# Row sums of a masked attention moved from POOL additions to a ScalarE exponential, and the next input loaded into dead buffers

## The reference, cut to what matters

```
f0: norm_adj @ (x @ W) + bias                          # norm_adj = d^-1/2 adj d^-1/2
f1: 8 heads of 32; softmax over q.k/sqrt(32) where adj != 0, else -inf;
    @ v @ w_proj + b; plus a scaled layernorm of that result
f2: 3 steps of a gated unit: a = adj @ h; z, r = sigmoid(..); h = (1-z) h + z tanh(..)
f3: 8 heads of 32; softmax over q.k/sqrt(32) - 1e9 (1 - adj); @ v @ Wo + b
```

## Time and profile before

| what | value |
|---|---|
| median of 3 runs | 2841.97 us |
| lowest and highest | 2840.41, 3499.7 us |
| profiled execution | 2836.56 us |
| its span, first to last instruction | 2834.8 us |
| mean granted TensorE clock | 0.967 |

### The profile page before, as it was taken

The page is one execution under the profiler, slowest core; times in us unless marked ns, Lnnn a source line. Parts: engine busy times, 40 slices in busy tenths (PEclk is TensorE's granted clock), DMA queues, the critical chain, the costliest instruction groups (busy, mean ns, idle before and its releaser), DMA issues.

```text
span 2834.8 us, 50080 instructions
## 1 busy us (share of the span) xinstructions
PE 2594.9 (92%) x16825; PEld 2007.0 (71%) x16825; DVE 2463.6 (87%) x5962; ACT 1686.0 (59%) x3559; POOL 1474.8 (52%) x1787
## 2 busy tenths in 40 slices
PE   7878989999999998989989899998989989898997
PEld 6556767777776776767777677777767777676775
DVE  7978889899898988989899898998988889889676
ACT  4434755748466574755747467474665746545677
POOL 2756456445745546565455654446555464657312
PEclk8889999999999999999999999999999999999999
DMA  5211202212031121202212031121301222021022
GB/s 142 45 26 23 59 18 61 50 38 59 20 77 31 38 59 47 65 18 50 59 40 59 18 68 42 39 59 34 69 26 37 59 53 59 18 48 36 12 46 68
DMA packets 93231, 132.80 MB, mean 47 GB/s; under 512 B 16977, under 2 KB 42226, under 8 KB 92978
## 3 DMA queue, kind: packets, MB, share of 16 engines
q1 hardware_dynamic: 92978, 129.60, 19.7%
HBM read 19.83 MB, written 8.39 MB: 10 GB/s over the span
## 4 chain that ended last, share of the span: by engine, by line
DVE 37%; PE 35%; POOL 15%; issue 9%; ACT 3%; SPq 1%; DMA 1%; POOLq 0%; DVEq 0%; ACTq 0%
DVE PT L1490 8%; PE bank L1728 7%; PE bank L1730 7%; PE bank L1729 7%; PE bank L1836 4%; POOL acc L1111 4%; POOL acc L1113 4%; PE bank L1782 3%; PE bank L1851 3%; DVE gate L1608 3%; POOL acc L1115 3%; DVE probs L1473 2%; DVE bank L1465 2%; DVE vh L1573 2%; DVE gate L1606 2%
## 5 line engine op out<-in xcount | busy, mean ns | idle before, releaser
L1490 DVE SCALAR_TENSOR_TENSOR PT<-adjT,PT 128x512 f32<-128x512 f32 x512 | 471.8, 969 | 49.3 <-ACT PT L1212 48.5
L1220 ACT ACTIVATE probs<-probs,few 128x512 f32<-128x512 f32 x512 | 367.5, 723 | 45.9 <-DVE few L1473 44.5
L1115 POOL TENSOR_TENSOR acc<-PT 128x256 f32<-128x256 f32 x256 | 240.3, 962 | 229.2 <-DVE PT L1490 219.1
L1465 DVE CUSTOM_DVE_ANT_0 bank<-bank,mask 128x512 f32<-128x512 f32 x512 | 344.7, 702 | 11.2 <-PE bank L1782 5.9
L1473 DVE CUSTOM_DVE_ANT_0 probs<-bank,mask 128x512 f32<-128x512 f32 x512 | 336.5, 684 | 15.1 <-PE bank L1836 9.3
L1212 ACT ACTIVATE PT<-bank 128x512 f32<-128x512 f32 x512 | 273.0, 599 | 119.6 <-PE bank L1805 103.9
L1836 PE MATMUL bank<-before_ident,probs 128*128 128x128 f32 x2048 | 302.2, 276 | 13.4 <-ACT probs L1220 5.5
L1782 PE MATMUL bank<-stack 96*128 96x512 f32 x768 | 282.7, 437 | 15.6 <-DMA stack<-qk 10.5
L1836 PEld LDWEIGHTS bank<-before_ident,probs 128*128 128x128 f32 x2048 | 236.0, 141 | 84.9 <-DVE few L1473 23.3
L1728 PE MATMUL bank<-feat,W 128*128 128x512 f32 x640 | 268.2, 419 | 7.8 <-DVE feat L1441 3.2
L1079 POOL TENSOR_TENSOR feat<-o,feat 128x256 fp32r<-128x256 f32 x128 | 101.7, 794 | 326.5 <-ACT feat L1249 326.5
(11 more groups left out here) (136 smaller groups left out, 6897.0 us busy)
## 6 DMA issues: line engine op xcount, KB each, us to landing
stack<-qk SPq DMA_DIRECT2D x576, 128.0 KB, 2.4
qk<-qk SPq DMA_DIRECT2D x192, 128.0 KB, 2.4
res<-in_x_dram SPq DMA_DIRECT2D x16, 512.0 KB, 3.8
out_dram<-res SPq DMA_DIRECT2D x16, 512.0 KB, 2.9
stack<-feat SPq DMA_DIRECT2D x192, 2.0 KB
rows<-bo_sum SPq DMA_DIRECT2D x15, 128.0 KB, 2.9
rows<-in_L_gnn_bias_dram SPq DMA_DIRECT2D x14, 128.0 KB, 3.0
rows<-in_L_gnn_ln_beta_dram SPq DMA_DIRECT2D x14, 128.0 KB, 3.0
```

Source lines behind the costliest of these rows:

```text
L1115: k = pool.tensor_tensor(to, first, second, ALU.add)
L1220: k = act.activation(p, p, ACT.Exp, bias=least[:, t % P_RING:t % P_RING + 1], scale=-1.0, accum_out=sums[:, later_at[grp] % 2, q * HG + h: ...
L1465: k = dve.tensor_tensor_reduce(out=place("scores", t)[:, :], in0=place("scores", t)[:, :], in1=mask1[:, q, :], scale=1.0, scalar=3.4e38, o ...
L1490: k = dve.scalar_tensor_tensor(p, adjT[:, HI, 2 * i:2 * i + 2, half * QH:(half + 1) * QH].bitcast(F32), 0.0, p, ALU.not_equal, ALU.min)
```

## The change

In words:

- After `shift` has put the masked scores into the bank, ScalarE takes their exponential in place with `row_least` as bias and a running sum (`sum_row`), in `first_sums`, a ring of two units. The exponentials themselves are not used. The scores bank is free after this, and a new scores tile comes behind the sum of the third before instead of its minimum.
- `add_up` and the buffers `acc0` and `acc1` go. The first attention gets its factors as the second does: one reciprocal for both groups of a unit, POOL's spread, two transposes by TensorE (`row_factors`), ScalarE's copy, the multiply. The reciprocal over 128x256 goes. The second-pass exponential no longer waits for additions, nor `shift_hi` for the first head group's values.
- x of batch b + 3 is loaded by two DMAs into `x_in`, a part of `qk` that is dead when the second attention of batch b has its last stacks; scaling, `ax` and the bias addition work from there in queues of their own ("front"). `ax` is moved out of its bank only after the last projection of batch b; `w0` reads `x_in`, writes `res` and waits for the store of batch b.
- The second attention's projection (`proj3`) is ordered behind a late minimum of its batch. `UNITS` has (3, 13, 0) ahead of (1, 15, 1) in place of behind it. `RANK` is a new table (not shown), with kinds of their own for the first 32 tiles. Nominal costs of removed pieces go, `mask` has 0.68 for 0.61. The scratch size for DMAs is 512 for 1024.

```diff
-        if b >= STREAMS:
-            add(sp, "SP", ("load", b), ("store", b - STREAMS))
+        early = b >= STREAMS
+        pe_x, act_x, dve_x, pool_x, sp_x = (("front", *of) if early else of for of in (pe, act, dve, pool, sp))
+        if early:
+            add(sp_x, "SP", ("load", b), *[("stack", 3, b - STREAMS, 1, h) for h in range(HG)])
         for t in range(NT):
-            add(act, "ACT", ("act", "scale", b, t), ("load", b), ("prep", "DVE", "dinv"))
-            add(dve, "DVE", ("dve", "scale", b, t), ("act", "scale", b, t))
-        add(*((dve, "DVE") if b < STREAMS else (pool, "POOL")), added("scale", b), ("dve", "scale", b, NT - 1),
+            add(act_x, "ACT", ("act", "scale", b, t), ("load", b), ("prep", "DVE", "dinv"),
+                *([("stt", last_of_head(3, b - STREAMS, 1, 0))] if early else []))
+            add(dve_x, "DVE", ("dve", "scale", b, t), ("act", "scale", b, t))
+        add(*((pool_x, "POOL") if early else (dve, "DVE")), added("scale", b), ("dve", "scale", b, NT - 1),
             ("row", row_at["scale", b]))
         for f in range(FT):
-            add(pe, "PE", ("pe", "ax", b, f), ("dve", "scale", b, NT - 1), ("prep", "DVE", adjs[-1]), opens=[("ax", b, f)])
-            evacuated(b, ("ax", b), f)
+            add(pe_x, "PE", ("pe", "ax", b, f), ("dve", "scale", b, NT - 1), ("prep", "DVE", adjs[-1]), opens=[("ax", b, f)])
+            evacuated(b, ("ax", b), f, *([("pe", "proj3", b - STREAMS, NT // 2 - 1)] if early else []))
         for tp in range(NT // 2):
             add(pe, "PE", ("pe", "w0", b, tp), ("dve", "ax", b, FT - 1), ("prep", "DVE", "lo_w0"),
                 opens=[("w0", b, tp)])
             add(dve, "DVE", ("dve", "w0", b, tp), ("pe", "w0", b, tp), added("scale", b),
-                frees=[("w0", b, tp)])
+                *([("store", b - STREAMS)] if early else []), frees=[("w0", b, tp)])
...
+            sums_read = [("rsum", read), ("rsum", read + 1)] if read is not None else []
+            older = least_before(t)
+            add("stt1", "DVE", ("stt", t), ("scores", t), *([("sum", older)] if older is not None else []))
+            add("sum1", "ACT", ("sum", t), ("stt", t), *sums_read, frees=[("scores", t)])
             if row % GROUP == GROUP - 1:
                 hp = row // GROUP
                 add("shift", "PE", ("minT", b, g, hp), ("stt", t), opens=[("minT", b, g, hp)])
-                add("shift", "ACT", ("neg", b, g, hp), ("minT", b, g, hp), ("act", "v", b, 1, NT // 2 - 1),
-                    *([("values", group_at(1, b, HALVES - 1), PARTS - 1)] if g else []))
+                add("shift", "ACT", ("neg", b, g, hp), ("minT", b, g, hp), ("act", "v", b, 1, NT // 2 - 1))
                 add("shift", "DVE", ("neglo", b, g, hp), ("neg", b, g, hp), frees=[("minT", b, g, hp)])
                 add("shift", "SP", ("negrow", b, g, hp), ("neglo", b, g, hp))
...
             add("mask", "DVE", ("mask", t), ("exp", t))
-            add("padd", "POOL", ("padd", grp, in_columns(t)[1], i), ("mask", t),
-                *([last] if grp % HALVES else []))
             if t % GROUP == GROUP - 1:
+                if half == 0:
+                    add("recip1", "DVE", ("recip", grp), ("sum", grp * GROUP + SIDE - 1))
+                add("rsum", "POOL", ("rsum", grp), ("recip", grp - half),
+                    *([("pool", "out3", grp - 1)] if grp else []))
                 for part in range(PARTS):
-                    done = part == PARTS - 1
                     add("values", "PE", ("values", grp, part), ("mask", grp * GROUP + (part + 1) * HG - 1),
-                        *([("padd", grp, HG - 1, 1)] if done else []), ("act", "v", b, layer, NT // 2 - 1),
-                        opens=() if part else [("values", grp)], takes=SUMMED_US[part])
+                        *([("rsum", grp)] if part else []), ("act", "v", b, layer, NT // 2 - 1),
+                        opens=() if part else [("values", grp)])
...
-            if layer == 1:
-                add("out_dve", "DVE", ("dve", "out1", grp), ("values", grp, PARTS - 1),
-                    *([("pool", "out3", grp - 1)] if grp else []), frees=[("values", grp)], takes=FIRST_LAYER_US["out1"])
-            else:
-                add("out", "ACT", ("act", "out0", grp), ("values", grp, PARTS - 1))
-                add("out_dve", "DVE", ("dve", "out1", grp), ("act", "out0", grp), frees=[("values", grp)])
+            add("out", "ACT", ("act", "out0", grp), ("values", grp, PARTS - 1))
+            add("out_dve", "DVE", ("dve", "out1", grp), ("act", "out0", grp), frees=[("values", grp)])
...
         qn = [qk[j][:, 0, :, :] for j in js]
         ka = [qk[j][:, 1, :, :].rearrange("p s (f n) -> p s f n", f=FT) for j in js]
 
-        stats = [gate[j][:, 0, 0, 0:6 * NT].rearrange("p (t c) -> p t c", t=NT) for j in js]
+        x_in = [qk32[j][:, 1, :, N:2 * N].rearrange("p s (u d) -> p s u d", u=NT // 2) for j in js]
+        stats = [qk32[j][:, 1, 0, 0:6 * NT].rearrange("p (t c) -> p t c", t=NT) for j in js]
...
                     if b >= STREAMS:
-                        sp.wait_ge(stored[b % STREAMS], b // STREAMS * 16)
-                    sp.dma_start(res[b % STREAMS][:, :, :], x_v[b]).then_inc(x_loaded[b % STREAMS], 16)
+                        for h in range(HG):
+                            at, loads = loads_of(3, b - STREAMS, 1, h)
+                            sp.wait_ge(stacked[at], loads)
+                        for i in range(2):
+                            sp.dma_start(x_in[b % STREAMS][:, i, :, :],
+                                         x_v[b][:, i * NT // 2:(i + 1) * NT // 2, :]).then_inc(x_loaded[b % STREAMS], 16)
+                    else:
+                        sp.dma_start(res[b][:, :, :], x_v[b]).then_inc(x_loaded[b], 16)
...
             def sums_of(grp):
                 if grp:
 
                     layer, b, gh = half_of(grp - 1)
                     wait_sig(pool, out_lo[b % STREAMS], f"o{layer}{gh}", b)
-                pool.wait_ge(recip_ready.sem, recip_ready.at(grp))
+                if grp in later_at:
+                    pool.wait_ge(recip_ready.sem, recip_ready.at(grp))
+                else:
+                    pool.wait_ge(first_recip.sem, first_recip.at(grp - grp % HALVES))
                 i = pool.tensor_tensor(rsum.rearrange("p q (h d) -> p (q h) d", h=HG),
-                                       sums[:, later_at[grp] % 2, :].unsqueeze(2).broadcast_to([P, QT * HG, HD]),
+                                       group_sums(grp).unsqueeze(2).broadcast_to([P, QT * HG, HD]),
                                        one[:, :].unsqueeze(2).broadcast_to([P, QT * HG, HD]), ALU.mult)
                 rsum_ready.raised_by(i, grp)
...
+            def sum_row(t):
+                layer, b, g, *_ = tile_of(t)
+                h, q = in_rows(t)
+                act.wait_ge(shifted1.sem, shifted1.at(t))
+                read = sums_before(b, g)
+                if h == 0 and q == 0 and read is not None:
+
+                    for grp in (read, read + 1):
+                        act.wait_ge(rsum_ready.sem, rsum_ready.at(grp))
+                p = place("scores", t)[:, :]
+                k = act.activation(p, p, ACT.Exp, bias=row_least[:, least_at(h, q):least_at(h, q) + 1], scale=-1.0,
+                                   accum_out=first_sums[:, side_at[b, g, 0] % SUMS_RING, q // QT,
+                                                        q % QT * HG + h:q % QT * HG + h + 1])
+                first_summed.raised_by(k, t)
...
-                dve.wait_ge(exped3.sem, exped3.at(grp * GROUP + GROUP - 1))
-                k = dve.reciprocal(sums[:, later_at[grp] % 2, :], sums[:, later_at[grp] % 2, :])
-                recip_ready.raised_by(k, grp)
+                if grp in later_at:
+                    dve.wait_ge(exped3.sem, exped3.at(grp * GROUP + GROUP - 1))
+                    k = dve.reciprocal(group_sums(grp), group_sums(grp))
+                    recip_ready.raised_by(k, grp)
+                else:
+                    layer, b, g, *_ = tile_of(grp * GROUP)
+                    dve.wait_ge(first_summed.sem, first_summed.at(grp * GROUP + SIDE - 1))
+                    both = first_sums[:, side_at[b, g, 0] % SUMS_RING, :, :]
+                    first_recip.raised_by(dve.reciprocal(both, both), grp)
 
             def output(grp):
-                if grp in later_at:
-                    dve.wait_ge(rb_ready.sem, rb_ready.at(grp))
-                else:
-                    wait_full(dve, "values", grp)
-                    if grp:
-
-                        layer, b, gh = half_of(grp - 1)
-                        wait_sig(dve, out_lo[b % STREAMS], f"o{layer}{gh}", b)
-                    m = mark(dve.reciprocal(o32[:, :], place("values", grp)[:, QH:2 * QH]))
-                    wait_mark(m)
+                dve.wait_ge(rb_ready.sem, rb_ready.at(grp))
                 k = dve.tensor_tensor(o32[:, :], place("values", grp)[:, 0:QH], o32[:, :], ALU.mult)
```

(13 more changed lines are left out.)

160 lines of the change are left out of this document (81 added, 79 removed), and 14 rows, old and new, of the table RANK.

## The result

The changed kernel takes 2603.26 us (median of 4 runs, 2602.27 to 2604.86), 0.9166 of the kernel before, 95% interval 0.9148 to 0.9184 (one slow execution of the kernel before, 3499.7 us, left out). That is 8.3% faster; I had said 3.8%, and the range ended 47 us above the measured time.

The account below looks back on a forecast made before the run. TensorE (92% busy) was taken as nearly full, idling where POOL adds the first attention's exponentials. 2834.8 less 120 idle and 15.5 busy, plus 30 new, gave 2729 us of span, stated as 2735 (-3.8%), range 2650 to 2820.

Parts of the forecast that it names:

- floor: TensorE's busy time after the change, 2579 us, taken as a least time for the kernel.
- the first rival: Whole kernel: VectorE was the real bound and TensorE's 92% is stretchable; 2655 us, chance 0.13.
- ScalarE's sums: First attention's scores banks: 512 sums hold banks longer, +25 us, and evacuations wait behind sums, +5.
- The bound of 471: Scores banks: at most 512 x 0.92 = 471 us if each longer hold for a sum reaches TensorE.
- the slow rival: Scores banks: TensorE waits for banks that ScalarE holds for the sums; 2905 us, chance 0.07.
- half of three VectorE waits: TensorE's waits of 41.9 (gated state), 16.2 and 8.4 us for late VectorE: half goes, 33 us.
- the early load: Load of x for batch b + 3: TensorE's wait for the scaled x goes whole, 27.2 us.
- The check against the windows: Steady stretch: POOL-full windows hold 14.2/15.3 of its 163 us idle, 151; the 120 forecast is most of it.
- VectorE's 100 us for the masks: First attention's 512 mask multiplies: 100 us of VectorE saved, of 143 at most, without POOL's additions.
- the factor chain: First attention's factors: POOL's spread, transposes, ScalarE's copy, VectorE's multiply; between 0 and 39 us, taken as 0.
- The order: Last units interleaved differently and hand-out order computed anew: at most 3.8 + 15.1 us behind 2600 us, taken as 0.
- The second (the idle only moves): Whole kernel: a released wait exposes the next, so only 49 us are gained; 2793 us, chance 0.18.

## Why the prediction was wrong

The sign held, and with it that the additions and the masks they stretch were the largest loss; the size did not, by 128 us of span (2729 forecast, 2600.9 measured). Of these, 81 are TensorE's busy time and 47 its idle.

**TensorE's busy time is no floor: 81 of the 128 us.** This is the step that failed. The sum had 2579 and it is 2498. I had written of the 2579 that it "is a floor", and bounded the first rival with it: even with the idle that was measured, 102.6 us, it gives 2682, inside the range. The matmuls themselves ran slower before. Here is TensorE in the kernel before, behind one of the 13 waits for the scaled x (start us, duration us):

```profile
572.47 0.77 PE L1728 MATMUL bank<-adjT,qk 128*128 128x512 f32 x1 [2.79 <-DVE qk L1536]
573.03 0.63 PE L1729 MATMUL bank<-adjT,qk 128*128 128x512 f32 x1
573.46 0.63 PE L1730 MATMUL bank<-adjT,qk 128*128 128x512 f32 x1
...
577.73 0.63 PE L1728 MATMUL bank<-adjT,qk 128*128 128x512 f32 x1
...
578.53 0.39 PE L1730 MATMUL bank<-adjT,qk 128*128 128x512 f32 x1
578.76 0.40 PE L1728 MATMUL bank<-adjT,qk 128*128 128x512 f32 x1
578.99 0.40 PE L1729 MATMUL bank<-adjT,qk 128*128 128x512 f32 x1
```

After 2.79 us of idle the 128x512 products start 0.43 us apart, at 1.2 GHz; from 578.5 on they are 0.23 apart, at 2.4. Fourteen of them lost about 0.2 us each, 2.8 us: this wait cost twice its length. Not every wait does: at 1600.10 us the same product follows a wait of 2.80 us and the next ones start 0.23 us apart at once, while at 1161.31 one of 1.48 us is followed by products 0.43 apart.

Over the whole span the clock's share can be estimated from the mean: 2834.8 x (1 - 0.967) = 94 us of full-speed time lost before, 2600.9 x (1 - 0.989) = 29 after, 65 us regained. That also counts low clock while TensorE was idle, which costs nothing; slices of 2 us over the whole span, each weighted by TensorE's busy time in it, give 78 and 21, 56 us regained. The run without additions agrees: 51 us by such slices (78 to 27), of a busy time that fell by 62. The sum had this at nothing, though 0.98 stood in the earlier trace rows and I named it as a point for the first rival. The other 16 to 25 of the 81 us stay open; the ends of matmuls are modelled.

**The idle: 47 us, 28 of them the sums.** The forecast took 120 us of idle away and put 30 back for ScalarE's sums, 90 net; 137 went, 239.9 to 102.6. The sums' waits for banks are 1.8 us, and all that they cost is 10 us at most. The bound of 471 was real as an upper end, but TensorE nearly always had another bank; the slow rival had no ground. Without the 30 the forecast would be 17 us of idle short.

**Whose the idle was.** I gave the additions 35.9 us for L1828, 24.1 behind the masks, and half of three VectorE waits, 93 in all, and the early load the 27.2 for the scaled x. Left out alone, with the load still late, the additions take 127 us of idle with them (239.9 to 113.3), the 27.2 among them, and then the busy time: 188 us. So 120 was near the right total for the wrong parts. The check against the windows gave 151 for the steady stretch; 116 of its 163 went (2117 less 2069.8 is left). The windows pointed at the right engine, but their idle was an upper end.

POOL as a queue is a further cost in the runs with the additions put back and the order kept. In the kernel before no row shows it: TensorE's direct waits for the remainders (L1079, L1096) are 5.5 us there and 4.6 without the additions.

**What of it collides.** Of VectorE's 100 us for the masks only 36 came (471.8 to 435.3 busy); the gated step's five operations gave 91 (423 to 331), where I had 40. Without the additions but in the old order it was the other way round, 127 and 27: which of the two meets the POOL operations that stay depends on the order. The total was right by luck (246 forecast, 253 measured). That two SBUF operands beside a reading POOL are the cause is shown by the run with the exponential in the bank and the one with POOL's writes.

The Trainium skill's "SBUF — State Buffer", section "Who interferes with whom", has it so: a VectorE instruction with at most one SBUF input, outside the modes that use two ports, doesn't contend. The measurement agrees (665 to 690 ns).

**The reciprocal** got no TensorE time of its own. It is worth 16 to 19 us in an order made for it, 65 to 70 in one that isn't.

**The early load** had 27 us, the direct wait alone, and that wait was not the load's: it is 1.0 us without the additions, with the load still late. What the load is worth stays open. With searched tables for the new work it is 97 us (51 of idle, 45 of busy time), from one search each. The other way round, the kernel before without additions and reciprocal, with late load and the order kept, takes 2632; the changed kernel without its sums takes 2594. Of these 38 us some 11 are the row-of-ones products, which the first still has (TensorE busy 67.8 us for these and the transposes, against 56.5), so about 27 are left for the load and the new order together, if the rest of the factor chain is free. That the load was undersized is therefore not shown.

**The order** I took at 0. Its tail is next to 0: TensorE idles 1.3 and 14.9 us in the last two windows, 3.8 and 15.1 before. But the new table is needed: with the old one the change gives nothing at all (0.9999). I don't count it as a gain beside the others, since the old kernel had a table of its own; that the old table was as good for the old work as the new one is for the new isn't shown. It can't be most of the gain, since 188 us came with the old order kept.

The first rival (VectorE the real bound, 2655) came nearest in time with the wrong reason: 112 us of VectorE are worth 16 to 70. The second (the idle only moves) fell: the gated step's wait, its main point, went from 41.9 to 1.1 us. The range failed because every case in it stood on the same floor.

## What to carry to other kernels

Where one engine at 93% loses its time in the windows in which another is full, don't price the removal by the waits that name that engine alone (35.9 us here, of 127 that went): waits put down to a third engine can be its doing too, if its operations are stretched beside it. The idle of those windows is an upper end (151 us here, 116 came). A TensorE wait with slow matmuls behind it costs those too, so read the rows that follow it; and a busy time at a mean clock below 1 is not a floor. An engine that is half idle can still be late for everyone if its queue is in order and long operations stand before short ones (105 us of TensorE's waits in the run with the additions put back); and when an order was fitted by hand or search, test a part with the order kept, or fit both sides.

## What the runs showed of the hardware

- The mask multiply on VectorE with two SBUF operands: 656 to 2920 ns beside POOL's work; with one operand in a bank: 665 to 690. POOL's constant writes, 956 us of them, didn't raise its mean (770 beside them, 887 in the changed kernel); its additions, put back, brought it to 960 to 1043. The scaling of x, 128x256 with two SBUF operands, had a median of 939 ns with the additions and 473 without.
- A wait of 2.79 us on TensorE was followed by 5.7 us at 1.2 GHz, in which 128x512 products came 0.43 us apart instead of 0.23; one of 2.80 us at another place was followed by full clock, and one of 1.48 us by a slow stretch.
- ScalarE's exponential from a bank back into the same bank, with a running sum, took 657 ns and 201 for the sum; from SBUF to SBUF 717 and 192.
